# A transformer layer on eight cores: the affine step of the layer norm moved from GpSimd to VectorE, and the softmax exponentials taken over two PSUM groups at a time

## The reference

```python
xn = layernorm(x)                      # no affine part
def lora_linear(x, W, b, Bm, Am):      # rank 16, scaling 0.5
    return x @ W.T + b + 0.5 * (x @ Bm.T) @ Am.T
q, k, v = (split_heads(lora_linear(xn, ...)) for the three of them)
attn = softmax(q @ k.T * 128 ** -0.5)          # 4096 x 4096 per head
att  = lora_linear(merge_heads(attn @ v), Wo, bo, Bo, Ao)
u    = layernorm(xn) * gamma + beta
ffn  = (sign(u) @ sign(weight - weight.mean(1)).T + bias) * alpha
out  = x + att + ffn
```

## Time and profile before

| | us |
|---|---|
| median of 2 runs | 8736.49 |
| lowest and highest | 8658.39, 8814.59 |
| profiled execution, its own time | 8660.23 |
| its span on the slowest core (core 1) | 8658.7 |
| spans of the eight cores | 8643.6 to 8658.7 |
| granted TensorE clock, mean of the span | 0.85 |

### The profile page before, as it was taken

How to read it: one execution, slowest core, us unless ns; L and a number is a source line. 1 busy time by engine, 2 the same in 40 slices (tenths; PEclk the granted TensorE clock), 3 DMA queues, 4 the chain that set the end, 5 groups by cost and what they waited for, 6 DMA issues and landing times. The chain is left out here.

```text
span 8658.7 us, 69870 instructions; the slowest of 8 cores (8643.6 to 8658.7 us)
## 1 busy us (share of the span) xinstructions
PE 5637.9 (65%) x23096; PEld 2171.9 (25%) x23096; DVE 3101.1 (36%) x2814; ACT 2551.6 (29%) x2487; POOL 291.3 (3%) x81
## 2 busy tenths in 40 slices
PE   1111168888888866666666666666666665996499
PEld 0111133333333322222222222222222222332243
DVE  2333311111111134444444444444444444112433
ACT  1222200000000045555555555555555553000100
POOL 1222200000000000000000000000000000000000
PEclk9999998888989877777777777777777776998699
DMA  1111111111111110000000000000000002443344
GB/s 35 49 50 47 54 44 56 57 51 57 53 55 53 45 37 19 19 19 19 5 19 19 19 19 5 19 19 19 19 19 5 19 4 85 155 148 112 118 169 151
DMA packets 171889, 425.10 MB, mean 49 GB/s; under 512 B 26005, under 2 KB 107925, under 8 KB 142869
## 3 DMA queue, kind: packets, MB, share of 16 engines
q1 hardware_dynamic: 80922, 269.60, 9.4%
q10 hardware_dynamic: 90624, 151.02, 4.7%
HBM read 269.58 MB, written 150.99 MB: 49 GB/s over the span
## 5 line engine op out<-in xcount | busy, mean ns | idle before, releaser
L766 ACT ACTIVATE pT<-sg,negc 128x1024 bf16<-128x1024 f32 x2048 | 2098.2, 1140 | 1706.8 <-DVE ostg L602 1505.0
L776 PE MATMUL avp<-pT,vh 128*128 128x512 bf16 x4096 | 1318.6, 405 | 570.9 <-ACT pT L766 570.8
L744 PE MATMUL sg<-qT,kT 128*128 128x512 bf16 x4096 | 1292.2, 410 | 0.0
L787 DVE TENSOR_TENSOR ptree<-pT 128x4096 bf16<-128x4096 bf16 x128 | 293.4, 2292 | 1769.4 <-ACT pT L766 1769.4
L502 PE MATMUL pgA<-xn_fm,wT 128*128 128x512 bf16 x3072 | 727.8, 399 | 25.2 <-DVE wT L487 25.2
L502 PE MATMUL pgB<-xn_fm,wT 128*128 128x512 bf16 x3072 | 726.6, 399 | 25.3 <-DVE wT L487 25.3
L776 PEld LDWEIGHTS avp<-pT,vh 128*128 128x128 bf16 x4096 | 312.6, 101 | 1576.1 <-issue 1540.3
L810 DVE TENSOR_TENSOR ptree<-ptree 128x4096 bf16<-128x4096 bf16 (+3 forms) x512 | 593.1, 1158 | 63.4 <-DVE ptree L802 22.4
L744 PEld LDWEIGHTS sg<-qT,kT 128*128 128x128 bf16 x4096 | 421.3, 103 | 591.4 <-issue 175.4
L665 ACT ACT_TABLE_LOAD x1 | 1.3, 1283 | 1878.1 <-DMA qT<-s_qT 1878.1
L617 PE MATMUL avp<-ptree,ones_bfc 128*1 128x512 bf16 x128 | 75.0, 586 | 722.5 <-DVE obuf L614 722.5
(11 more groups left out here) (125 smaller groups left out, 3596.6 us busy)
## 6 DMA issues: line engine op xcount, KB each, us to landing
xf<-x SPq DMA_DIRECT2D x32, 1024.0 KB, 4.8
x_sp<-x SPq DMA_DIRECT2D x32, 1024.0 KB, 6.5
out<-res ACTq DMA_DIRECT2D x64, 512.0 KB, 3.9
ord<-out SPq DMA_DIRECT2D x32, 1024.0 KB, 6.5
out<-res4b ACTq DMA_DIRECT2D x64, 512.0 KB, 4.4
s_a<-a_acc ACTq DMA_DIRECT2D x16, 1024.0 KB, 5.1
wbuf<-wq SPq DMA_DIRECT2D x16, 1024.0 KB, 6.1
wbuf<-wk SPq DMA_DIRECT2D x16, 1024.0 KB, 6.0
```

The costliest lines, as they stand in the source:

```text
L744: ins = nc.tensor.matmul(sg3[b][:, j * 512:(j + 1) * 512], kT_b[sl][:, kt * 128:(kt + 1) * 128], qT_b[sl][:, qq0:qq0 + 512], start=True, s ...
L766: e = ac.inc(nc.scalar.activation(pT2[qsl][:, g * 1024:(g + 1) * 1024], sg3[s_bank[g]][:], AF.Exp, bias=negc2[sl].ap()))
L776: pe.inc(nc.tensor.matmul(avp[qsl][:], vh2[sl][:, kt * 128:(kt + 1) * 128], pT2[qsl][:, kt * 512:(kt + 1) * 512], start=(kt == 0), stop=(k ...
L787: tree_a[0] = dv.inc(nc.vector.tensor_tensor(ptree2[qsl][:, 0:wq // 2], pT2[qsl][:, 0:wq // 2], pT2[qsl][:, wq:wq + wq // 2], ALU.add))
```

## The change

Two edits. In stage 1 the two operations with gamma and beta go from GpSimd to VectorE, in the same place of the source: VectorE issues them behind its second normalisation and ahead of the copies of the transposes; the waits for GpSimd go. In stage 3 the three PSUM tiles become three slices of one tensor `sgall`, and the loop over groups takes two groups in one 2048-column exponential where the first is not in tile 2 and the second is in the next tile. TensorE then waits for that exponential, and issues `AV(g)`, `S(g+3)`, `AV(g+1)`, `S(g+4)`. Where that is not so, a group goes alone as before.

```diff
                 if t >= 1:
-                    nc.vector.wait_ge(gpc.h, gpc.v)
                     nc.vector.wait_ge(ac.h, prev_sign[0])
...
-                nc.gpsimd.wait_ge(dv.h, v_u)
-                nc.gpsimd.wait_ge(gpc.h, gpc.v)
-                gpc.inc(nc.gpsimd.tensor_tensor(xn32.ap(), xn32.ap(), gb_g.ap(), ALU.mult))
-                nc.gpsimd.wait_ge(gpc.h, gpc.v)
-                v_b = gpc.inc(nc.gpsimd.tensor_tensor(xn32.ap(), xn32.ap(), gb_b.ap(), ALU.add))
-                nc.scalar.wait_ge(gpc.h, v_b)
+                nc.vector.wait_ge(dv.h, v_u)
+                v_g = dv.inc(nc.vector.tensor_tensor(xn32.ap(), xn32.ap(), gb_g.ap(), ALU.mult))
+                nc.vector.wait_ge(dv.h, v_g)
+                v_b = dv.inc(nc.vector.tensor_tensor(xn32.ap(), xn32.ap(), gb_b.ap(), ALU.add))
+                nc.scalar.wait_ge(dv.h, v_b)
...
-    sg3 = [es_p3.enter_context(nc.psum_tensor(f"sg3{i}", [128, 1024], F32)) for i in range(3)]
+    sgall = es_p3.enter_context(nc.psum_tensor("sgall", [128, 3072], F32))
+    sg3 = [sgall[:, i * 1024:(i + 1) * 1024] for i in range(3)]
...
-                    for g in range(NKG):
-                        nc.scalar.wait_ge(pe.h, s_done[g])
+                    g = 0
+                    while g < NKG:
+                        fuse = (g + 1 < NKG and s_bank[g] != 2
+                                and s_bank[g + 1] == s_bank[g] + 1)
+                        span = 2 if fuse else 1
+                        nc.scalar.wait_ge(pe.h, s_done[g + span - 1])
...
                         e = ac.inc(nc.scalar.activation(
-                            pT2[qsl][:, g * 1024:(g + 1) * 1024], sg3[s_bank[g]][:],
+                            pT2[qsl][:, g * 1024:(g + span) * 1024],
+                            sgall[:, b0 * 1024:(b0 + span) * 1024],
                             AF.Exp, bias=negc2[sl].ap()))
-                        bank_waits[s_bank[g]].append((ac, e))
+                        for gg in range(g, g + span):
+                            bank_waits[s_bank[gg]].append((ac, e))
                         nc.tensor.wait_ge(ac.h, e)
...
+                        for gg in range(g, g + span):
...
-                        if g + 3 < NKG:
-                            emit_S(g + 3, s_done, s_bank, q0)
+                            if gg + 3 < NKG:
+                                emit_S(gg + 3, s_done, s_bank, q0)
+                        g += span
```

More of the change, by code:

```diff
@@ L765, in _ @@
                             nc.scalar.wait_ge(dv.h, negc_ready[sl])
+                        b0 = s_bank[g]
                         e = ac.inc(nc.scalar.activation(
-                            pT2[qsl][:, g * 1024:(g + 1) * 1024], sg3[s_bank[g]][:],
+                            pT2[qsl][:, g * 1024:(g + span) * 1024],
+                            sgall[:, b0 * 1024:(b0 + span) * 1024],
                             AF.Exp, bias=negc2[sl].ap()))
-                        bank_waits[s_bank[g]].append((ac, e))
+                        for gg in range(g, g + span):
+                            bank_waits[s_bank[gg]].append((ac, e))
                         nc.tensor.wait_ge(ac.h, e)
@@ L773, in _ @@
                                 nc.tensor.wait_ge(dv.h, avfree[qsl])
[L774 to L789, removed]
@@ L790, in _ @@
-                        if g + 3 < NKG:
-                            emit_S(g + 3, s_done, s_bank, q0)
+                        for gg in range(g, g + span):
+                            for j in range(2):
+                                kt = 2 * gg + j
+                                pe.inc(nc.tensor.matmul(
+                                    avp[qsl][:], vh2[sl][:, kt * 128:(kt + 1) * 128],
+                                    pT2[qsl][:, kt * 512:(kt + 1) * 512],
+                                    start=(kt == 0), stop=(kt == NT - 1),
+                                    skip_group_check=True))
+                            if gg == (3 * NT // 4 - 1) // 2:
+                                wq = NT * 256
+                                if ptree_mm[qsl]:
+                                    nc.vector.wait_ge(pe.h, ptree_mm[qsl])
+                                nc.vector.wait_ge(ac.h, e)
+                                with nc.allow_low_precision(reason="bf16 tree partials (softmax sums; final 128-way sum in fp32 PSUM)"):
+                                    tree_a[0] = dv.inc(nc.vector.tensor_tensor(
+                                        ptree2[qsl][:, 0:wq // 2], pT2[qsl][:, 0:wq // 2],
+                                        pT2[qsl][:, wq:wq + wq // 2], ALU.add))
+                            if gg + 3 < NKG:
+                                emit_S(gg + 3, s_done, s_bank, q0)
```

## The result

The changed kernel is slower: 9351.45 us median of 11 runs (9238.59 to 9587.83), 1.069 times the kernel before, 95% interval 1.060 to 1.078. The forecast was 9235 us, 6.6% more; the profiled execution took 9327.93 us, with a span of 9326.4 us on core 1 and 9227 to 9235 on cores 4 to 7. In part of the executions of every kernel here, before included, some cores are granted a third clock level, 0.81, for hundreds of us in place of 1.00, so stages are compared on cores that have little or none of it, such as core 4 here.

A forecast was written before the change was run, and what follows sets the result against it. ScalarE was taken to bound stage 3 between a chunk's first and last exponential, while stage 1's sign waited for GpSimd. 8660 - 145 (stage 1) + 720 (stage 3) = 9235 us, 6.6% more; range 9130 to 9420.

The forecast's parts named there:

- The ring: Stage 3: wide exponential, eight matmuls refilling its two tiles, next wide exponential; 4.20 us for three groups, which took 3.0.
- The body: Stage 3, a chunk's first to last exponential on ScalarE: forecast to grow from 17.2 to 22.8 us in cold chunks.
- The later rise that was allowed for: Stage 3 chunks: 0.3 us added to the mean of 22.5 for TensorE's clock rising later than before.
- The 112 later chunks: Stage 3 chunks that begin with a cold clock: forecast to grow 5.6 us each, 627 us together.
- The 16 first chunks: Stage 3, each head's first chunk, taken as all warm: 22.1 us against 16.19, 94 us together.
- The tail: Stage 3, after a chunk's last exponential: ScalarE idles behind VectorE's sums, reciprocal and scaling; forecast to stay 13.46 us.
- Stage 1: Gamma and beta operations on VectorE at 2.29 us each: path 4.9 us instead of 9.42, 145 us gained over 32 tiles.
- The sum: Whole kernel: 8660 - 145 + 720 = 9235 us, 6.6% more; the median of two runs perhaps nearer 9300.
- ScalarE did not stay the bound: Rival, 3%: in stage 3 ScalarE stays the bound, three groups cost 2.86 us instead of 3.0; kernel faster, 8411 us.
- this rival: Rival, 6%: TensorE's clock falls inside stage 3's chunks; 10,170 us if cold, about 9,700 if it flips back and forth.
- The wide exponential didn't cost two: Rival, 10%: stage 3's wide exponential costs two narrow ones, 0.26 us more each, 166 us in all; 9400 us.

## Why the prediction was right

- *The ring.* 4.20 us forecast, 4.21 measured, each part of it as priced: the wide exponential 1.97 (1.96), `AV` 0.15 behind it, seven starts, 0.21 to ScalarE. The runs with `S` first show that what stands between two pairs, and nothing about the width, sets it.
- *The body.* Forecast 23.0, 21.6 and 23.0 us for chunks that begin with tile 1, 2 and 0 at the old rise of the clock; the means on core 4, without the heads' first chunks, are 23.2, 22.1 and 23.0. The later rise that was allowed for came: on core 4 the clock rose 4.4 us behind a chunk's first `AV` in the mean (2.7 to 6.0), where it had been 3.3 on core 1 of the kernel before. The 0.3 us put down for it, an unworked estimate, was about right in size and belongs mostly to chunks that begin with tile 2: in the rows above their second pair starts 6.9 us in (5334.38), forecast 6.0, behind matmuls that are still cold. Stage 3 grew by 728 us on core 4, forecast 720.
- *Some luck in that total.* The 112 later chunks of the heads grew by 617 us on core 4, forecast 627; their mean was forecast with shares of 3, 3 and 2 in 8, where it is 2, 3 and 2 in 7 without the first chunk (22.4 instead of 22.5). The 16 first chunks grew by 110 us, forecast 94: they were taken as warm throughout at 22.1 us, and have a mean of 23.4. Seven of them began at a clock of 0.50, and in four the clock fell to it inside the body. The two misses have opposite signs.
- *The tail.* 13.46 us (the median of every core), untouched.
- *Stage 1.* 2 x 2.29 + 0.3 = 4.9 against 4.88; 147 us against 145. The price from the sum over 2048 columns was right to a hundredth (2.29). The figure of the Trainium skill (GPSIMD Engine Reference, 3.1), 2293 ns, which no row of before could show, agrees.
- *The sum.* 9235, against 9235.4 on core 5 and 9238.6 in the fastest run. That the two agree to 1 us is luck in part, since small misses in both stages stand behind it. The median lies 1.3% above; the prediction had left room for that as the distance of the profiled execution to its median.
- *The rivals.* ScalarE did not stay the bound, it idled 1.23 us a ring. The clock stayed up inside the body of 124 of the 128 chunks on core 4, though TensorE idled 1.46 of every 4.21 us. In the other four, each the first chunk of a head, it did fall: in the one that starts at 5699.26 us the granted clock is 1.00 from 5700 to 5702 and 0.50 from 5704 to 5708, 6.8 us in all, and the body took 24.0 us against 22.2 to 22.6 in the five first chunks that had 1.00 throughout. So this rival was real but small, some 6 us of the 728 (4 x 1.6). The Trainium skill (TensorE: Matmul & The Clock Gate, A second HAM failure mode: psum-queue depth-cycling) says that small idle gaps between groups of matmuls cycling through PSUM make the clock swing; the one fall in each of four chunks is all that this trace has of it. The wide exponential didn't cost two.

What the prediction had not seen is how much of the loss lies in the order: of the 711 us, 456 go when `S` is issued ahead of `AV` (4895 to 4439), and only the other 255 need the pairs off.

## What to carry to other kernels

Before merging two instructions that read rotating buffers, walk the ring: the wide one, whatever its consumer does before the buffers are refilled, the refill, and back. If that exceeds what the wide engine needs for the whole rotation, the merge makes a bound out of what was slack; refilling first and consuming second shortens the ring for nothing. And where an engine waits for one thing, look for a second wait behind it before pricing its removal: 13.46 us of wait were worth 1.6.

## What the runs showed of the hardware

- TensorE idled 1.46 us of each ring of 4.21 us, and the granted clock read 1.00 through the rest of the body once it was up, in 124 of 128 chunks on core 4. In four first chunks of a head it fell to 0.50 some 3.4 us into the body and stayed there for 6.8 us.
- The rise of the clock behind a chunk's first `AV` moved with the pattern of TensorE's work: 3.3 us in the mean before (core 1), 4.4 us with the pairs (core 4), there between 2.7 and 6.0.
- An exponential from PSUM took 1.11 us for 1024 columns, 1.54 for 1536 and 1.97 for 2048, and the next could begin 0.11 us before its end.
- The handover from an exponential's end to TensorE was 0.15 us in one order and 0.25 in the other.
- The multiplication and the addition of 128x2048 fp32 took 4.50 and 4.49 us on GpSimd and 2.29 us each on VectorE.
